# A fused patch, state-space and gated-attention kernel: the same instructions in another hand-written order of units, with other PSUM banks

## The reference

```
tok:  x = LN(patches @ patch_w + b) + pe            # 16 x 64 tokens x 192
      x = attn12(gelu_tanh(x@ff1)@ff2) + x ; x = gelu_tanh(x@ff1)@ff2 + x
h = concat(x, txt)                                  # 16 x 96 tokens x 192
attn: y = LN(h); y += (silu(conv4(xb)) * silu(z)) @ out_proj    # xb, z = LN(y) @ in_proj
      y += attn12(LN(y)) @ proj ; y += gelu(LN(y)@ffn1)@ffn2 ; h = h + y
ffn:  LN(h); gates = softmaxes, top 2 of 10 experts
      q, k, v of 12 heads of 64, q and k layer-normed; o = gates * attn(q, k, v); h + o @ proj
```

## Time and profile before

| | |
|---|---|
| median of three runs | 611.57 us (609.36 to 615.26) |
| the profiled execution | 607.84 us, span 606.0 us |
| PE busy | 541.3 us, 89% of the span |
| DVE busy | 434.4 us, 72% |
| ACT busy | 293.1 us, 48% |
| POOL busy | 70.4 us, 12% |
| mean granted TensorE clock | 0.954 |

### The profile page before, as it was taken

The page is one execution under the profiler, slowest core; times in us unless marked ns, Lnnn a source line. Parts: engine busy times, 40 slices in busy tenths (PEclk is TensorE's granted clock), DMA queues, the critical chain, the costliest instruction groups (busy, mean ns, idle before and its releaser), DMA issues.

```text
span 606.0 us, 10532 instructions
## 1 busy us (share of the span) xinstructions
PE 541.3 (89%) x4337; PEld 408.5 (67%) x4337; DVE 434.4 (72%) x878; ACT 293.1 (48%) x392; POOL 70.4 (12%) x72
## 2 busy tenths in 40 slices
...
PEclk9899799967999999999998999999987999999889
...
DMA packets 12673, 15.99 MB, mean 26 GB/s; under 512 B 6235, under 2 KB 10048, under 8 KB 12240
## 3 DMA queue, kind: packets, MB, share of 16 engines
...
q0 software_dynamic: 512, 0.59, 0.5%
...
## 4 chain that ended last, share of the span: by engine, by line
PE 43%; DVE 25%; issue 17%; SPq 6%; ACT 4%; DMA 3%; POOL 2%; ACTq 0%; DVEq 0%; POOLq 0%
PE ps L993 8%; PE ps L680 8%; PE ps L1051 4%; PE ps L690 4%; DVE smax L1666 4%; DVE pr L1668 4%; PE ps L670 3%; SPq L557 3%; DMA w_cproj<-in_cproj 3%; PE ps L1041 2%; DVE psum L1677 2%; PE ps L1160 2%; PE ps L813 2%; DVE pr L1689 2%; DVE ss L1768 1%
## 5 line engine op out<-in xcount | busy, mean ns | idle before, releaser
L1666 DVE TENSOR_REDUCE smax<-ps 96x12 f32<-96x1152 f32 x32 | 43.2, 1349 | 25.9 <-PE ps L1041 17.5
L1341 ACT ACTIVATE pr<-pr 96x1152 f32<-96x1152 f32 x28 | 32.6, 1163 | 48.0 <-DVE pr L1668 48.0
L1051 PE MATMUL ps<-w_ident,pr 96*96 96x96 f32 x336 | 35.4, 259 | 9.5 <-DVE pr L1689 6.7
L1051 PEld LDWEIGHTS ps<-w_ident,pr 96*96 96x96 f32 x336 | 30.3, 133 | 16.6 <-DVE pr L1689 9.1
L1347 ACT ACTIVATE pT<-ps 96x1152 f32<-96x1152 f32 x28 | 31.5, 1126 | 19.8 <-PE ps L1051 19.8
L1677 DVE TENSOR_REDUCE psum<-pr 96x12 f32<-96x1152 f32 x28 | 37.6, 1341 | 2.6 <-ACT pr L1341 2.5
L1668 DVE TENSOR_TENSOR pr<-ps,smax 96x1152 f32<-96x1152 f32 x28 | 37.9, 1354 | 1.0
L1374 ACT ACTIVATE squares<-ps 128x1536 f32<-128x1536 f32 x12 | 17.4, 1452 | 28.2 <-PE ps L690 21.2
L670 PE MATMUL ps<-w_cqkv,side_c 128*96 128x384 f32 (+1 forms) x96 | 27.6, 505 | 1.6 <-DVE pr L1668 1.6
L1041 PE MATMUL ps<-b_kB,heads 32*96 32x192 f32 x192 | 21.7, 397 | 8.0 <-ACT b_kB L1324 3.8
L1768 DVE TENSOR_REDUCE ss<-squares 128x24 f32<-128x1536 f32 x12 | 21.0, 1746 | 10.3 <-ACT squares L1374 10.3
...
## 6 DMA issues: line engine op xcount, KB each, us to landing
...
```

Of the source, the lines that this page charges most:

```text
L1051: m = pe.transpose(t[0:N, h // 4, (h % 4) * N:(h % 4 + 1) * N], w.y.pr[:, s % 2, h * N:(h + 1) * N], w_ident[0:N, 0:N])
L1341: act.activation(w.y.pr[:, s % 2, :], w.y.pr[:, s % 2, :], ACT.Exp, scale=head ** -0.5)\
L1666: dve.tensor_reduce(mx, t, AX.X, ALU.max).then_inc(w.S[stage + "_sub"], 1)
```

## The change

Only `STEPS_TEXT` changes. It has the same 419 units, so the same instructions but for the automatic ones (ACT table loads follow the order of functions). The order of words, the bank numbers, and through them `NARROW_FIRST` for 12 products, are new. The complete old and new text is long; these are the stretches that the prediction speaks of (old, then new):

```diff
-    d_en:0 d_em:0 d_x0:0=7 warm.0=3 a_bc=5 a_en:1 d_f1.0:0=2 a_em:1=5 d_f2.0:0=1 d_h2.0:0 a_tb=5 a_x0:1=0 d_qk:0=3
-    d_ot.0:0 a_wc.0 d_o.1:0=3 d_ot.1:0=3 a_e.0:1 d_pr:0 a_s.0:1=1 d_f1.1:0=4 a_e.1:1 a_wc.1 a_s.1:1=0 d_f2.1:0
-    d_h2.1:0 a_pt.0:1 d_ht:0=0 a_v:1 a_o.0:1 a_pt.1:1 d_u:0=0 a_wc.2 a_ot.0:1=7 a_o.1:1=3 d_in.0:0 a_pb a_ot.1:1
-    d_cv.0:0 d_cv.1:0 a_pr:1 d_in.1:0=2 d_cv.2:0 d_gt.0:0 a_f1.1:1 d_gt.1:0 d_gt.2:0 d_out.0:0=4 d_out.1:0
-    d_out.2:0=1 a_f2.1:1=3 a_h2.1:1=5 b_u.1:0 a_ht:1=2 b_qk:0 a_u:1 b_v:0=2 b_e.0:0 b_s.0:0 warm.1=3 b_s.1:0 b_e.1:0
...
-    b_f2.1:0 b_f2.2:0=2 warm.2=7 c_u:0=3 b_u.1:1=0 c_g:0=6 a_en:2 b_qk:1 a_em:2 b_s.0:1 b_v:1 a_x0:2 b_e.0:1
...
-    a_pt.0:2=2 a_s.1:2=5 b_pt.3:1=2 a_o.0:2=7 a_e.1:2 b_pr.1:1 a_pt.1:2 b_o.3:1=7 a_ot.0:2 a_o.1:2 c_qk.0:0=3
-    a_ot.1:2=6 c_qk.1:0 a_pr:2 b_pr.2:1=6 c_qt.0:0 c_qk.2:0 c_qt.1:0 c_v.0:0 a_f1.1:2 c_s.0:0 a_f2.1:2 b_u.2:1
...
-    c_pr.2:1 b_u.1:3=2 b_qk:3=4 warm.3 b_s.0:3=2 b_s.1:3 b_n.0:3 b_e.0:3 b_e.1:3 e_u:2=1 b_v:3 b_pt.0:3 b_n.1:3
...
-    c_qk.1:3=3 c_qk.2:3 c_v.0:3=3 c_qt.0:3=5 c_qt.1:3=2 c_s.0:3=5 c_e.0:3 c_s.1:3 c_e.1:3 c_n.0:3 c_v.1:3=6 c_n.1:3
-    c_qt.2:3 c_pt.0:3 c_s.2:3 c_o.0:3=6 c_n.2:3 c_pt.1:3 c_e.2:3 c_v.2:3=6 c_s.3:3 c_o.1:3=6 c_v.3:3=0 c_pr.0:3
+    d_em:0=4 d_en:0 warm.1=7 d_x0:0=4 a_bc=3 a_en:1 d_f1.0:0 a_em:1 d_f2.0:0=3 d_h2.0:0 a_x0:1=1 d_qk:0 a_f1.0:1=1
+    d_e.0:0 d_s.0:0=6 d_v:0=4 a_f2.0:1=2 d_s.1:0 d_pt.0:0=3 a_h2.0:1=7 d_e.1:0 d_o.0:0=6 d_pt.1:0=2 a_qk:1=4 a_tb
+    d_ot.0:0=3 d_o.1:0=1 a_wc.0 d_ot.1:0 d_pr:0=7 a_e.0:1 a_s.0:1=4 a_wc.1 d_f1.1:0=0 d_f2.1:0=5 d_h2.1:0=6 a_e.1:1
+    a_s.1:1=3 a_pt.0:1 d_ht:0=5 a_v:1=3 a_o.0:1 a_pt.1:1=5 d_u:0 a_ot.0:1 a_wc.2 d_in.0:0=0 a_pb a_o.1:1=4 a_ot.1:1
+    d_in.1:0=4 d_cv.0:0 d_cv.1:0 a_pr:1=2 d_gt.0:0 d_gt.1:0 d_cv.2:0 a_f1.1:1 d_gt.2:0 d_out.0:0 d_out.1:0=2
+    d_out.2:0=7 a_f2.1:1=3 a_h2.1:1=6 b_u.1:0=3 a_ht:1 b_qk:0=3 a_u:1=6 b_e.0:0 b_s.0:0 b_s.1:0=5 b_n.0:0 b_e.1:0
+    b_n.1:0 b_v:0 a_in.0:1 b_pt.0:0 b_s.2:0 b_e.2:0 a_in.1:1=4 a_cv.0:1 b_n.2:0 b_o.0:0 b_pt.1:0=0 b_e.3:0 b_s.3:0=4
...
+    b_f2.0:0 b_f2.1:0=1 b_f2.2:0=2 a_em:2=3 c_u:0=1 a_en:2 c_g:0=1 b_qk:1=4 a_x0:2 b_v:1 b_s.0:1 b_s.1:1=0 warm.0=6
...
+    b_pr.0:1 b_o.2:1 a_e.1:2 a_o.0:2 b_pt.3:1 a_pt.1:2=5 a_ot.0:2=3 b_pr.1:1 a_o.1:2 c_qk.0:0 c_qk.1:0=3 c_v.0:0=6
+    a_ot.1:2=1 c_qt.0:0=3 a_pr:2=7 c_qk.2:0=0 b_o.3:1=6 a_f1.1:2 c_qt.1:0 b_pr.2:1=4 c_v.1:0 c_s.0:0 a_f2.1:2=5
...
+    b_o.1:2=2 c_v.0:1 b_pt.2:2=2 b_n.3:2 a_e.0:3 a_s.1:3 b_o.2:2=4 a_pt.0:3=2 b_pr.0:2 b_pr.1:2=7 a_e.1:3 a_o.0:3=6
...
+    a_out.1:3=0 a_out.2:3=2 c_pr.2:1=7 b_u.1:3=1 e_u:2 b_qk:3 b_s.0:3=1 b_s.1:3 b_n.0:3 b_e.0:3 warm.3=3 b_e.1:3
...
+    e_e.3:2 e_pr.0:2=4 e_n.3:2 e_v.3:2=5 e_pt.2:2 b_f2.2:3=4 e_o.2:2 e_pt.3:2=0 e_pr.1:2=6 e_o.3:2=2 e_pr.2:2=1
+    c_u:3 c_g:3=7 c_qk.0:3 c_qk.1:3 c_qk.2:3 c_qt.0:3 c_qt.1:3 c_s.0:3=3 c_s.1:3 c_e.0:3 c_e.1:3 c_n.0:3 c_n.1:3
+    c_qt.2:3=5 c_v.0:3=3 c_v.1:3=0 c_pt.0:3=5 c_s.2:3 c_n.2:3 c_o.0:3 c_pt.1:3=5 c_e.2:3 c_v.2:3=0 c_o.1:3 c_s.3:3
```

More of the change, by code:

```diff
@@ L84 @@
[L84 to L88, removed]
```

39 lines of the change are left out of this document (20 added, 19 removed).

## The result

The changed kernel took **620.01 us** (median of 6 runs, 618.04 to 623.36), the kernel before 613.41 us beside it: a ratio of 1.0143, 95% interval 1.0093 to 1.0193. It is slower. I had forecast 608.8 us, with 617 as the upper end. The profiled execution took 619.34 us, 11.5 us more than that of before. So the two traces lie further apart than the medians (6.6 us): the trace of before was 5.6 us quicker than the median beside the changed kernel, the trace after 0.7 us.

What follows compares the result with a forecast made beforehand. PE (busy 89%, DVE 72%) was taken as the main limit, with only its 64.7 us idle and half-clock stretches to gain. Terms summed to -2.75 us: 607.84 to 605.1, plus 3.73 for a median of 608.8 us; range 601 to 617.

Steps and rivals of the forecast that it cites:

- warm.1 in the first idle stretch: Between d_em and d_x0: the product might keep the clock up; -0.7 us, from nothing to 3.0 us back.
- a_wc.0 behind d_o.1 and the clock at 58.7: At d_o.1: DVE takes it earlier, -0.65 us; the clock then does not fall from 58.7, -4.3 us.
- Rival (2): Clock falls at 58.7 as before, DVE's order gains only 0.65, last stage keeps its half clock; 613.6 us, chance 0.12.
- d_in.0 and d_in.1: Moved ahead of a_o.1 and a_pr: a_o.1 and a_pr's sum come later, a_f1.1 waits; +1.9 us, bounds 0 to +3.46.
- b_v of group 0: Moved behind b_s.0 and b_s.1: opens a PE gap, first scores take longer if the clock falls; +0.5 us (0 to +8.6).
- rival (3): Clock falls in the new gap before b_s.0:0, at 114 to 117, costing up to 8.6 us; 617.9 us, chance 0.10.
- Two more table loads: ScalarE switches 30 times instead of 28, 1.28 us each, covered ahead of its waits; 0, or +2.6 us uncovered.
- a_em fills the hole: a_em of group 2 fills PE's 2.75 us hole before c_u with 4.06 us of work; -1.2 us (0 to -2.75).
- The four holes of the attention part ... stay in number: Attention part before the first gated stage: its four PE holes, 4.6 us in all, stay equal in number; no term.
- First gated stage: c_v.0, c_v.1 moved forward and b_pr.2 behind c_qk.2: DVE idles, scores delayed, GpSimd stall goes; +2.7 us (-1.1 to +4.9).
- Rival (1): DVE not starved in the first gated stage, so only the -1.1 us of the vanished stall remains; 605.0 us, chance 0.30.
- Second gated stage: c_v.0 sits in a gap of the scores before it, leaving less work afterwards; -0.4 us (0 to -2.75).

Runs made afterwards that it cites:

- the first gated stage back: Changed kernel with its words from a_pt.1 of group 2 to c_g of group 1 in the old order; 623.21 us, ratio 1.0201.
- both attention parts back: Changed kernel with the attention parts of groups 1 and 2 in the old order and banks; 616.26 us, ratio 1.0093.

## Why the prediction was wrong, point by point

- **warm.1 in the first idle stretch**, -0.7: wrong size. The clock fell there all the same, from 16.9 to 23.8. The +1.26 isn't its cost either: kernels with the old start were 0 to 1.95 behind at d_qk, those with the new one 0.03 to 1.64. The effect can't be measured; three products there are worth 1.8 to 3.7 us.
- **a_wc.0 behind d_o.1 and the clock at 58.7**, -4.95: the place and the mechanism are right (wait 0.73 us, clock 1.00), and the -5.2 between the two traces is partly luck. I took the fall of one trace, 10.2 us, as the kernel's; three other traces with a_wc.0 in its old place fall for 3.4 to 6.8 us, and against them the changed kernel's stretch gains 1.6 to 2.8. Alone, the move gave a ratio of 1.0014. Rival (2) had "the clock falls at 58.7 as before"; that happened in one of twelve traces with the move (from 58.9 to 62.3, the first gated stage back).
- **d_in.0 and d_in.1**, +1.9: measured +1.8.
- **b_v of group 0**, +0.5 with a bound of +8.6: +1.6. The gap opened as rival (3) says (2.64 us in front of b_s.0), and 0.50 stood from 115.9 to 119.3 and again from 136.4 to 153.5. It cost little because DVE decides there, as I had argued, until the low stretch reached past DVE's work into b_pr and b_o, where DVE was busy 13.04 of 17.10 us instead of 15.99.
- **Two more table loads**, 0: no run isolates them. The page has the two more instructions on ScalarE (394 against 392). At eight of the loads in either trace only 1.31 us pass from the end of one ACTIVATE to the start of the next, 1.28 of them the load, so the drain of about 1.38 us that I had counted as possible doesn't show there.
- **a_em fills the hole**, -1.2: failed, +0.1 up to b_n.1 of group 1. c_u's releaser was on DVE, so filling the hole moves nothing. And I didn't price the hole that a_em leaves: 1.38 us of waiting for ScalarE's keys. What it costs in all stays open, since in three of the four traces with the old words this stretch is itself 2.9 to 4.4 us slower than in the one that I compare with.
- **"The four holes of the attention part ... stay in number"**, 0 for groups 1 and 2: the step that failed, and it stands for most of the error. I put it at nothing, without bounds. It measured 5.1 us in each (of group 2's, 1.7 us are given back in the next stage, see below). I counted the words moved (a_h2 in front of b_s.2, a_v in front of b_s.3, c_v.0) as neutral because the same work was done. The runs showed it otherwise. In group 2's part old words lose nothing (1.4 us with c_v.0 moved), new words 1.6 to 1.9 us at a held clock and 4.2 to 7.1 with a fall. In group 1's, idle products in the gaps, and a free bank for the old one, cut the loss from 5.1 to 0.5, so that there it was nearly all clock. Which of the moved words opens the gaps isn't shown; a_h2 and a_v, put back, don't close them.
- **First gated stage**, +2.7: +3.7, right in kind. b_pr.2's place alone makes as much; I had the wait for the squares (2.71 us, forecast 2.7) and the vanished stall, and missed the bank wait. Rival (1), at 0.30, is refuted: DVE was starved and nothing was caught up. The loss is the same 3.7 us in five other traces with these words.
- **Second gated stage**, -0.4: -2.1. With both attention parts back, and c_v.0 with them, the new words of this stage gained 0.4 us, as forecast; so 1.7 of the 2.1 come with c_v.0's work, paid in the attention part. Moved alone, into the old words, it brought nothing here.
- **Group 3, e_u, e_pr, last stage**, -0.6 together: +0.4. c_s.2 did run at the full clock and DVE's wait behind it shrank, as TensorE and VectorE of the changed kernel show against the earlier trace rows, and the stage still lost 0.2, since the clock fell earlier in it, at 573.3 and 583.5:

```profile
590.46 1.26 PE L1160 MATMUL ps<-side_k,side_q 64*96 64x96 f32 x24
...
596.33 1.35 DVE L1677 TENSOR_REDUCE psum<-pr 96x12 f32<-96x1152 f32 x1 [1.82 <-ACT pr L1341]
```

The side that I gave 0.10 was the right one, and its mechanism was not the one that decided, so that its 617.9 us came near by luck. By its own words it should have been less: 8.6 us were added on top of the forecast's +0.5 for the same place, and DVE's slack of 1.1 us was not taken off. What would "upset the sum most", as I wrote at the end, was what did.
